# Cross-attention on one core: key stacks split for four heads in one instruction each and brought to their partitions through a scratch in memory

## The reference

```python
NH, NKV, HD, R, SCALING = 32, 8, 32, 16, 2.0
def lora(x, W, A, B): return x @ W + SCALING * (x @ A @ B)
q = lora(x, Wq, Aq, Bq)          # 32 query heads of 32
k = lora(ctx, Wk, Ak, Bk)        # 8 key heads of 32, each for 4 query heads
v = lora(ctx, Wv, Av, Bv)        # 8 value heads
attn = softmax(q @ k.T / sqrt(HD))
out = x + lora(attn @ v, Wo, Ao, Bo)
```

## Time and profile before

| | |
|---|---|
| time, median of 3 runs | 1073.62 us (1071.17 to 1074.78) |
| span of the profiled execution | 1069.5 us (4.1 us under the median) |
| PE busy | 997.3 us, 93% |
| DVE, ACT, POOL busy | 582.0, 496.0, 286.3 us |
| key stack on ACT (L977) | 121.4 us in 256 instructions |
| key stack on DVE (L1173) | 70.0 us in 128 instructions |

### The profile page before, as it was taken

One profiled execution on the slowest core, in us unless ns is written; L12 is line 12 of the kernel. 1 busy time (PEld: TensorE's weight loads), 2 busy tenths in 40 slices (PEclk: granted clock), 3 DMA queues, 4 the chain that ended last, 5 costly groups with the idle time before them and its releaser, 6 DMA issues.

```text
span 1069.5 us, 17947 instructions
## 1 busy us (share of the span) xinstructions
PE 997.3 (93%) x5904; PEld 787.8 (74%) x5904; DVE 582.0 (54%) x1005; ACT 496.0 (46%) x971; POOL 286.3 (27%) x84
## 2 busy tenths in 40 slices
PE   6988899959999999999999999999999877999998
PEld 5878799958777777777777777777777533678886
DVE  5660213237766666666666666666666565233331
ACT  3340212234566666666666666666666544200100
POOL 1201000000344344344344344344344355300000
PEclk9999899979999999999999999999999959999999
DMA  6827342272223333333332332332331333567552
GB/s 189 233 78 200 126 149 77 78 179 76 66 94 99 68 93 96 67 93 92 71 93 91 73 93 88 75 93 87 77 93 38 84 112 84 142 206 235 183 170 78
DMA packets 104052, 118.13 MB, mean 110 GB/s; under 512 B 29152, under 2 KB 88672, under 8 KB 104016
## 3 DMA queue, kind: packets, MB, share of 16 engines
q1 hardware_dynamic: 100156, 103.99, 35.4%
q10 hardware_dynamic: 3860, 13.67, 3.5%
HBM read 87.59 MB, written 29.82 MB: 110 GB/s over the span
## 4 chain that ended last, share of the span: by engine, by line
PE 74%; DVE 7%; ACT 6%; DMA 6%; issue 4%; SPq 2%; ACTq 0%; POOL 0%; DVEq 0%; POOLq 0%
PE ps L663 11%; PE ps L664 11%; PE ps L665 11%; PE ps L853 9%; PE ps L868 8%; PE ps L842 7%; PE ps L748 4%; PE ps L803 3%; PE ps L805 3%; PE ps L807 3%; PE ps L904 3%; DMA ctx_in<-in_ctx_dram 2%; DMA q_scratch<-q_out_lo 2%; ACT probs L1037 2%; DMA out_dram<-residual 1%
## 5 line engine op out<-in xcount | busy, mean ns | idle before, releaser
L1246 DVE TENSOR_REDUCE maxima<-ps 112x1 f32<-112x375 f32 x512 | 271.0, 543 | 107.8 <-PE ps L853 101.1
L1037 ACT ACTIVATE probs<-ps 125x448 f32<-125x448 f32 x384 | 206.8, 543 | 132.8 <-PE ps L842 128.6
L644 POOL TENSOR_TENSOR prob_sum<-probs 125x1792 f32<-125x1792 f32 x32 | 129.2, 4039 | 391.8 <-ACT probs L1037 391.8
L853 PE MATMUL ps<-k_stack,q_stack 96*112 96x376 f32 x512 | 190.2, 372 | 7.0 <-DVE maxima L1246 5.5
L842 PE MATMUL ps<-q_stack,k_stack 97*125 97x448 f32 x384 | 147.9, 385 | 10.5 <-ACT probs L1037 10.2
L853 PEld LDWEIGHTS ps<-k_stack,q_stack 96*112 96x112 f32 x512 | 91.6, 179 | 85.8 <-DVE maxima L1246 69.0
L649 POOL TENSOR_TENSOR prob_sum<-prob_sum,probs 125x1792 f32<-125x1792 f32 x32 | 129.0, 4032 | 32.6 <-ACT probs L1037 32.5
L977 ACT ACTIVATE k_stack<-ps 32x376 fp32r<-32x376 f32 x256 | 121.4, 474 | 10.0 <-PE ps L665 6.1
L803 PE MATMUL ps<-wv_hi,ct_hi 128*125 128x256 f32 x384 | 112.6, 293 | 0.5 <-DVE k_stack L1173 0.5
L1168 DVE TENSOR_TENSOR ct_lo<-ps,ct_hi 128x375 fp32r<-128x375 f32 x128 | 70.2, 549 | 76.2 <-ACT ct_hi L970 75.6
L807 PE MATMUL ps<-wv_hi,ct_lo 128*125 128x256 f32 x384 | 108.4, 282 | 0.0
(11 more groups left out here) (80 smaller groups left out, 1465.4 us busy)
## 6 DMA issues: line engine op xcount, KB each, us to landing
ctx_in<-in_ctx_dram SPq DMA_DIRECT2D x16, 1500.0 KB
q_stack<-q_scratch SPq DMA_DIRECT2D x96, 224.0 KB, 4.3
x_in<-in_x_dram SPq DMA_DIRECT2D x8, 896.0 KB, 9.3
q_scratch<-q_out_hi SPq DMA_DIRECT2D x16, 448.0 KB, 2.8
q_scratch<-q_out_lo SPq DMA_DIRECT2D x16, 448.0 KB, 3.7
attn_scratch<-attn SPq DMA_DIRECT2D x32, 224.0 KB, 4.5
attn_rows<-attn_scratch SPq DMA_DIRECT2D x14, 512.0 KB, 4.9
inv_tile<-inv_scratch SPq DMA_DIRECT2D x56, 128.0 KB, 5.1
```

Of the source, the lines that this page charges most:

```text
L644: pool.tensor_tensor(prob_sum[:, :, :], probs[:, 0, :, :], probs[:, 1, :, :], ALU.add).then_inc(psum_added, 1)
L853: mm = pe.matmul(ps[0:NQ, NAT + i % 2, 0:NTE], qst[nxt][0:STK, g, rr * NQ:(rr + 1) * NQ], kst[nxt][0:STK, g, :], start=True, stop=True)
L1037: act.activation(probs[:, c, j, :], ps[0:TR, score_bank(i), 0:QH], ACT.Exp, scale=SM).then_inc(exp_done, 1)
L1246: dve.tensor_reduce(maxima[:, h, i:i + 1], ps[0:NQ, NAT + i % 2, 0:NT], AX.X, ALU.max).then_inc(max_done, 1)
```

## The change

ACT makes the high part of all four heads of a key half in one instruction over 128 partitions, into a new tile `kev_hi`, and DVE the low part in one, into `kev_lo`, where E00, F00, E10 and F10 stood. SP then stores both tiles to a DRAM scratch (`store_k`, two transfers of 188 KB) at F00 and F10, and at F03 and F13 loads the stack from there (`load_k`, three transfers of 188 KB: high, high, low), once the stores have landed. N0 waits for these loads. ACT's wait for the last query stores moves from after step -1 to ahead of step -2.

```diff
+            def store_k(b, half):
+                sp.wait_ge(k_lo_set, 2 * b + half + 1)
+                for hl, t in ((0, kev_hi[half]), (1, kev_lo[half])):
+                    sp.dma_start(k_scr[hl, bass.ds(b, 1), half, :, :].rearrange("b p n -> p (b n)"),
+                                 t[:, :].bitcast(F32)).then_inc(k_stored[half], 16)
+            def load_k(b, par, half):
+                sp.wait_ge(k_stored[half], 32 * (b + 1))
+                for n, hl in enumerate((0, 0, 1)):
+                    sp.dma_start(kst[par][HD * n:HD * (n + 1), half * JH:(half + 1) * JH, :].bitcast(F32),
+                                 k_scr[hl, bass.ds(b, 1), half, :, :].rearrange("b (j d) n -> d (b j) n", d=HD)
+                                 ).then_inc(k_in[half][par], 16)
...
+                        elif kind == "F0" and i == 0:
+                            store_k(b + 2, 0)
+                        elif kind == "F0" and i == JH - 1:
+                            load_k(b + 2, off % 2, 0)
+                        elif kind == "F1" and i == 0:
+                            store_k(b + 1, 1)
+                        elif kind == "F1" and i == JH - 1:
+                            load_k(b + 1, (off + 1) % 2, 1)
                         elif kind == "K" and i == 1 and k == 0 and "C" in has[h]:
                             sp.wait_ge(ct_turned, (b + 3) * KC)
                             load_ctx(b + 3)
...
-                    pe.wait_ge(k_lo_set, NKV * b)
+                    pe.wait_ge(k_lo_set, 2 * b)
...
-                                at_least(pe, k_lo_set, NKV * (b + 1) + JH)
+                                at_least(pe, k_lo_set, 2 * (b + 1) + 1)
...
-                                pe.wait_ge(k_lo_set, JH * (m + 1))
+                                pe.wait_ge(k_in[h][nxt], 48 * (pair + (off + 1) // 2 + 1))
...
-            def k_hi(b, par, half, j):
+            def k_hi(b, half):
                 act.wait_ge(k_done, 2 * b + half + 1)
-                at_least(act, st_done, NS * (2 * (b - 2) + half + 1))
-                for quad in range(2):
-                    op = act.activation(kst[par][HD * quad:HD * (quad + 1), half * JH + j, :],
-                                        ps[HD * j:HD * (j + 1), (VA, TURN)[half], 0:NTE], ACT.Copy)
-                op.then_inc(k_hi_set, 1)
+                at_least(act, k_stored[half], 32 * b)
+                act.activation(kev_hi[half][:, :], ps[:, (VA, TURN)[half], 0:NTE], ACT.Copy).then_inc(k_hi_set, 1)
...
-            def k_lo(b, par, half, j):
-                dve.wait_ge(k_hi_set, NKV * b + half * JH + j + 1)
-                dve.tensor_tensor(kst[par][2 * HD:3 * HD, half * JH + j, :],
-                                  ps[HD * j:HD * (j + 1), (VA, TURN)[half], 0:NTE],
-                                  kst[par][0:HD, half * JH + j, :], ALU.subtract).then_inc(k_lo_set, 1)
+            def k_lo(b, half):
+                at_least(dve, st_done, NS * (2 * (b - 2) + half + 1))
+                dve.wait_ge(k_hi_set, 2 * b + half + 1)
+                dve.tensor_tensor(kev_lo[half][:, :], ps[:, (VA, TURN)[half], 0:NTE], kev_hi[half][:, :],
+                                  ALU.subtract).then_inc(k_lo_set, 1)
```

More of the change, by code:

```diff
@@ L206, in xattn_kernel @@
         qev_lo, at = place("q_out_lo", [P, QG, RH, NQ], F32R, at)
+        x_end = at
         def staging(tag, at):
@@ L221, in xattn_kernel @@
         raw2, wsum2, ast2, bst2, at = staging("_o", r_x)
-        assert at <= top[0]
+        kev_hi, kev_lo = [None, None], [None, None]
+        for half in range(HALVES):
+            kev_hi[half], at = place(f"k_out_hi{half}", [P, NTE], F32R, at)
+            kev_lo[half], at = place(f"k_out_lo{half}", [P, NTE], F32R, at)
+        assert at <= top[0], (at, x_end, top[0])
         at_raw, at_hi, at_lo, inv, res = ([None, None] for _ in range(5))
@@ L244, in xattn_kernel @@
         q_scr = nc.dram_tensor("q_scratch", [2, B, HALVES, P, QH], F32, kind="Internal").ap()
+        k_scr = nc.dram_tensor("k_scratch", [2, B, HALVES, P, NTE], F32, kind="Internal").ap()
         at_scr = nc.dram_tensor("attn_scratch", [P, KC, ROWS], F32, kind="Internal").ap()
@@ L288, in xattn_kernel @@
         k_lo_set = sem("k_lo_set")
+        k_stored = [sem("k_stored0"), sem("k_stored1")]
+        k_in = [[sem(f"k_in{h}{par}") for par in range(2)] for h in range(HALVES)]
         v_done = sem("v_done")
@@ L1026, in step @@
                             ctx_hi(b + 2, i)
[L1027 to L1030, removed]
+                        elif kind == "E0" and i == 0:
+                            k_hi(b + 2, 0)
+                        elif kind == "E1" and i == 0:
+                            k_hi(b + 1, 1)
                         elif kind == "S":
@@ L1071, in wo_factors @@
             def wo_factors():
-                for par in range(2):
-                    act.wait_ge(q_stored[par], GROUPS * QS // 2 * 32)
                 ab_hi(W_O, CTX)
+            for par in range(2):
+                act.wait_ge(q_stored[par], GROUPS * QS // 2 * 32)
             run_steps(act, step, wo_factors)
@@ L1239, in step @@
                             ctx_lo(b + 2, i)
[L1240 to L1243, removed]
+                        elif kind == "F0" and i == 0:
+                            k_lo(b + 2, 0)
+                        elif kind == "F1" and i == 0:
+                            k_lo(b + 1, 1)
                         elif kind == "N":
```

## The result

The changed kernel takes 1319.4 us (median of 4 runs, 1312.9 to 1323.65) against 1072.55 us before: a ratio of 1.231, 95% interval [1.226, 1.235]. The prediction said slower, by the queue of transfers, at 1270 us with a range to 1315. The direction and the place were right; the time lies 4 us above the range.

A forecast was written before the change was run, and what follows sets the result against it. PE was taken to bound the kernel. Terms: 18.1 (step -1) + 9.5 (step 0) + 182.0 (steps 1 to 13) + 2.4 (step 14) - 15.0 = 197.0 us on 1069.5, plus 4.1: 1270 us, range 1135 to 1315.

The forecast's parts named there:

- The key loads on the other 11 engines slow it as the query loads do now, by about 1 us: 514.7: Context load in each step: key loads beside it add about 1 us to its 11.7 us, ending at 514.7.
- The bounds: N0 of half 0 late by 11.3 us a step, between 8.5 (no slowing, fast tail) and 13.5.
- The tail: After the context, the key loads' share on its 5 engines takes 2.6 us, between 1.8 and 3.5.
- The undisturbed round trip: Key half 0's stores and loads with no context between them: N0 2.4 us late, bounds 1 to 3 us.
- The clock: After each step's 11 us idle wait PE runs at half clock: 2.7 us a step, bounds 0 and 3.4.
- The gain: PE's wait for ACT's exponentials in half 0 goes away: 1.0 us a step, 15 us over 15 steps.
- Half 1 is free: Key half 1's round trip of 10 us is hidden, its reader N0 coming some 20 us later; no cost.
- The start: Step -1: key stores wait for SP's query loads until 233.15, 18 us once; step 0: 6.8 us, with the clock 9.5.
- The key loads do not wait for the context: Rival for half 0: only latency counts, 1110 us, or 1135 if short waits also cost clock; chance 0.11.
- the round trip is hidden: Rival for half 0: transfers land within 6.2 us, N0 never waits; 1059 us, or 1077 with the start's 18; chance 0.06.
- The clock does not fall: Rival for PE after its waits: full clock in all or part of the steps, 1232 us; about a quarter of 0.77.
- the clock stays down for much of each step: Rival for PE: a half 0 at half clock costs 8 us and more a step, 1350 and above; chance 0.06.

The follow-up runs named there:

- experiment 2: Changed kernel with SP issuing the query loads of half 1 in the next half 0, behind the key stores: 1286.7 us, ratio 1.203.
- experiment 6: Changed kernel with the context load over 16 and 13 engines and issued behind the key loads: 1080.6 us, ratio 1.008.
- experiment 4: Changed kernel with 80 unused matmuls ahead of N0 in each half 0 from step 0 on, keeping PE busy: 1306.3 us, ratio 1.222.
- experiment 7: Changed kernel with only key half 1 through the scratch, key half 0 split as in the kernel before: 1055.0 us, ratio 0.984.
- experiment 1: Changed kernel with the context load issued behind the three key loads of key half 0 in SP's list: 1198.7 us, ratio 1.119.

## Why the prediction fell short

By N0's starts, before and after, the spans and the prediction's terms:

| stretch | forecast, us | measured, us |
|---|---|---|
| to N0 of step 0 | 18.1 + 6.8 - 1.0 = 23.9 | 289.89 - 265.69 = 24.2 |
| from there 13 steps | 13 x (11.3 + 2.7 - 1.0) = 169.0 | 739.6 - 521.8 = 217.8 |
| to the end | 197.0 - 192.9 = 4.1 | 241.6 - 242.0 = -0.4 |
| sum | 197.0 | 241.6 |

(521.8 is the same distance before, 265.69 to 787.44; 241.6 is the difference of the spans.)

- **The step that failed** is the sentence "The key loads on the other 11 engines slow it as the query loads do now, by about 1 us: 514.7". The mechanism was right and the term mis-sized: the time that the context needs. I had 11.7 + 1.0 = 12.7 us. From the first packet's start to the last one's it takes 16.8 in the mean of steps 1 to 13 (612.7 to 629.1 in the step shown). That is 4.1 of the 4.2 us by which the wait of 15.5 exceeds 11.3, and 13 x 4.2 = 55 us; the smaller clock term and the larger gain below give 6 of them back.
- **What the 4.1 us are.** The query loads, which SP issues right behind and which I had not counted at all, are 2.0 (16.8 against 14.8 in experiment 2). The key loads are 1.7 by the packet counts there, 0.7 more than allowed. The rest, 1.4, is by my estimate mostly a slow start, which the window of 498 to 505 in the earlier trace rows leaves out; what makes it slow is open. Of the kernel before, the packets in 496.2 to 498, all of them the context's, where 32 per us would give 58:

```profile
DMA packets 25, 0.10 MB, mean 57 GB/s; under 512 B 0, under 2 KB 0, under 8 KB 25
```

- **The row that would have priced it** was on record: in the kernel before the context is issued at 495.46 and its last packet starts in 510.2 to 511.2, at least 14.7 us later, where the sum has 1.0 + 12.7 = 13.7 for a context with more beside it.
- **The bounds failed with it.** With the longest tail, 3.5 us, the prediction's own terms give 12.2; its 13.5 leaves 1.3 us for all further slowing. The row for more was there: in 508.5 to 510.2 the context gets 18 packets through in 1.7 us, 11 per us, a third of its pace. The low bound doesn't come out of its terms either: no slowing and the fast tail of 1.8 give 9.5, not 8.5.
- **The tail**, 2.6 us, measured 2.8 in the mean (629.1 to 631.95 in the step shown). The undisturbed round trip, 2.4 us late, measured 2.99 in step 14, and 0.7 to 1.9 us in the steady steps of experiment 6. There it takes 7.7 us from the first store's issue to N0 (626.66 to 634.37) against the 8.5 of the forecast.
- **The clock**, 2.7 us a step: experiment 4 gives 2.2, and the sum 56.9 - 39.0 (step without these waits) - 15.5 gives 2.4.
- **The gain**, 1.0 us a step: 1.2 by experiment 7.
- **Half 1 is free**: shown by experiment 7.
- **The start**: 24.2 against 23.9 us at N0 of step 0, partly by luck. N0 and T0 of step -1 start within 1 us of the forecast, but PE has its full clock back sooner behind T0, so PE is 15.4 us late at the end of step -1 and not 17.1; the wait of step 0 adds 8.8 and not 6.8. The cause given, that SP is held in its query loads until 233, is only a part: in experiment 6 SP stores the keys at 213, and N0 of step -1 still waits 20.95 us, because the stores stand behind the context and nine query loads and land after 13.4 and 14.0 us.
- **The end** was 4.5 us better than forecast. N0 of step 14 comes 4.5 us later against N0 of step 13 than before, as it should, but from there to the end it is 237.3 us instead of 242.2. The granted clock of the first 40 us of that stretch is 0.96 instead of 0.83. Why is open; it is luck that it hid a tenth of the error in the steps.
- **The rivals.** "The key loads do not wait for the context" and "the round trip is hidden" fall with the waits of 15.5 us; the second falls in experiment 6 as well, where nothing of the context stands ahead and N0 still waits. "The clock does not fall" falls with the 0.50 of 620 to 634. That the clock stays down for much of each step was not seen.

## What to carry to other kernels

When a transfer is put on a path with a short deadline, read what is issued just ahead of it in the same queue and over how many engines that goes: here, with a context load on 5 of 16 engines ahead, N0 waited 15.5 us in every step, where it waited 0.7 to 1.9 with the context behind and on 16, and cutting the load into 112 and 13 partitions was worth 1.8% even to the kernel that never had the round trip. Price a large load from its issue to its last packet as the trace has it, slow start and contention included, and not by its best pace, and count every transfer that will share the time with it. Move through memory only what has its reader far away: the half whose reader comes 17 us after the first store won 1.2 us a step; the half with 6 us lost some 18, and still 1.5 with both cures.

## What was not expected of the hardware

- A load on 5 engines is slowed by transfers on the other 11: 32 packets of 4096 bytes per us alone, 23 beside the query loads, 14 beside the key loads.
- Engines take turns between SP's queue and ACT's (97 and 89 packets in 4 us), but here only after some 3.7 us (599.2 to 602.9) in which the context's queue had the 5 engines alone. Within one queue the later transfer's parts wait for the whole of the earlier (in the changed kernel 33 of 48 counts by 619.7, the other 15 from 629.7). Issuing the large load from the other queue spread the delay over all transfers here instead of removing it.
- Waits of 15.5 us brought the clock down in every step, and one of 6.4 us in the variant with 16 engines and one of 4.7 in experiment 1 did so as well; waits of 0.7 to 1.9 us in experiment 6 left the clock row of the page at 9 throughout the steady steps.
